# Half of a projection moved ahead, one wait added, and two banks for the last two tiles of a four-block network on one core

## The chip, the cores and the metric

The kernel runs on one NeuronCore of a Trainium2 chip, as one launch. The metric is the device time of the launch in microseconds, lower is better. The core has TensorE (PE, with its weight loads shown as PEld), VectorE (DVE), ScalarE (ACT), GpSimd (POOL), and SyncE (SP), which here issues nearly all DMAs. Each engine executes its own queue in order. They are tied together by semaphores that are waited on by value (`wait_ge`) and raised by instructions when they end (`then_inc`).

## The reference

Four blocks over a residual stream `x` of 1024 tokens by 256 channels, in float32:

```python
x = x + _layernorm(_L0_attn_ref(_layernorm(x), ...))   # softmax attention, 16 heads of 16
x = x + _layernorm(_L0_ffn_ref(_layernorm(x), ...))    # 8 experts, weights by a "golden zone"
x = x + _layernorm(_L1_attn_ref(_layernorm(x), ...))   # linear attention, 16 heads of 128
x = x + _layernorm(_L1_ffn_ref(_layernorm(x), ...))    # top 4 of 16 experts, and a shared one
```

The change touches the third block and the end of the fourth. The third, cut to its core:

```python
q, k, v = h @ Wq, h @ Wk, h @ Wv
beta, gate = sigmoid(h @ Wb + bb), silu(h @ Wg)
q = layernorm(silu(causal_dwconv(q, qconv_w, qconv_b)))    # 4 taps along the tokens, norm per head
k = layernorm(silu(causal_dwconv(k, kconv_w, kconv_b)))
S = (1 - b_t) * S + b_t * (v_t x k_t)                      # per token and head
o_t = S q_t
out = (o * gate) @ Wo
```

The fourth sums the down projections of all experts, weighted per token, over 2816 + 352 hidden rows; each token's sum of 256 channels is then normalised (mean and variance over the channels, eps 1e-5) and added to `x`, which is stored.

## The kernel before

Tokens lie in eight tiles of 128 (`NT = 8`). Channels of the residual stream lie along the free axis in `x` and, turned, along the partitions in `x_parts`. Matrices are multiplied in three matmuls, high x high, high x low, low x high, of operands that are split in two (`matmul3`, L62 to L67): ACT copies the high part to the narrower type, DVE or POOL subtracts it for the low part.

**The linear attention** (class `LinearAttention`, L1705) works head by head in a software pipeline. Head h's queries, keys, values and gates are projected (`project_half`: 512 tokens are six matmuls), convolved, activated, turned (PE transposes), normalised and then used in a chunked form of the recurrence: scores within each tile times a decay matrix `mix`, and states from tile to tile (`state`) times decayed queries `q_dec`. The decays come from one small computation for all heads at the start: logits `z`, their softplus (`exp_logit`, L2151, with the Exp and Ln tables of ACT), three small matmuls that sum them along the tokens (`sum_decay`, L1920), and three ACT operations that bring the sums out of PSUM (`decay_rows`, L2160). From there DVE makes the mix biases (L2340) and SP stores two arrays to DRAM and loads them again, broadcast, per head (`load_mix`, `load_decay`).

The order of each engine's work is written out by hand:

- PE (L2077 on): `finish_first`, the transposes of the first head's queries and keys (`rows_q(0)`, `rows_k(0)`), `sum_decay`, `second_q` (L1956: half of the second head's queries, the transpose of the first head's statistics, the other half), keys and values of the second head, and then the loop over heads: `rows_q`, `turn_k`, `rows_k`, gate, `score` (with the next statistics' transpose in its middle, L2009), `key_values`, the projections of the next head, `outputs`.
- ACT (L2241 on): taps and activations of the first head, `exp_logit`, `decay_rows`, a load of the Silu table, `tap_q(1)` (L2204, the two halves one after the other), `high_gate(0)`, the tap of the second head's keys, `norm_k(0)`, `silu_q(1)`, `copy_v(1)`, `silu_k(1)`, `exp_mix(0)`, and so on.
- DVE (L2476 on): convolutions of the first head, `logits`, `variances` of its queries (L2432: eight statistics, eight aggregates, one sum) with `decay_logs` behind, variances of its keys, `mix_biases`, `copy_stats(0)`, the convolutions of the second head with `shift_k(0)` in between, and so on. In the loop's first round: `probs(0)`, `states(0)`, `shift_k(1)`, the convolution of the third head's queries (L2405), `scale_q(1)` (L2464), the convolution of its keys.
- POOL (L2594 on): low parts of weights, powers for the reciprocal standard deviations, masks of the decay matrices (`mask`, L2547, an affine select over 1024 columns), decayed queries (`decay_q`, L2553), `centre_q` (L2536), the keys' rows. In the loop's first round (`n == 2`): low parts of q, `power`, low parts of k and v, `decay_q(0)`, `centre_q(1)`, `mask(2)`, low part of the gate, `rows_k(1)`, `decay_v(1)`.
- SP (L1844 on): behind `rows_ready` (the end of ACT's `decay_rows`) the stores of the sums, `load_mix(0)`, `store_stats(0)`, `load_norms(0)` (means, then rstds, broadcast from DRAM, for `centre_q` and `scale_q`), and then the loads of each round.

`shift_k` (L2345) is one DVE operation of 128x8 with two SBUF inputs, the keys' negative mean times rstd; `norm_k` on ACT waits for it through `shift_ready`. In L2632 before the change `decay_q(n - 2)` follows with no wait on it.

**The end** (`late_programs`, L2857; class `LastTail`, L2693). The down projections are summed in three passes over the token tiles, `PASSES = ((0, 4), (4, 2), (6, 2))`: tiles 0 to 3, then 4 and 5, then 6 and 7. A pass goes over 25 units (`NTILE`), tiles of hidden rows, and each unit adds `matmul3` for each of its token tiles (`sum_unit`, L3018). Two token tiles of 256 channels share one PSUM bank, `last.acc[j]`. ACT makes the high part of a unit (L3155), DVE the low part of odd units, POOL that of even ones (L3255, L3364). When a pair j of tiles is done, its tail runs: DVE takes statistics of both tiles, aggregates them and adds eps (`dve_first`, L975; `variance`, L960), POOL takes the power -1/2 (`pool_first`, L1007), DVE adds the scaled sums to `x` and makes the shift (`dve_take`, L2697), ACT adds the shift (`act_fix`, L1022), SP stores both tiles, 256 KB (L2997).

## Time and profile before

| | us |
|---|---|
| three runs before, median | 1043.86 |
| their lowest and highest | 1041.45, 1044.31 |
| the profiled execution, its own time | 1039.31 |
| its span, first to last instruction | 1037.5 |
| busy: PE | 1003.8 (97%) |
| busy: DVE, ACT, POOL | 768.5, 675.7, 535.7 |
| mean granted clock of PE, 1 = 2.4 GHz | 0.991 |

The profile is of one execution. Its page has, besides the busy times, the chain of work that ended last; PE has 56% of the span in it, DVE 6%, ACT 3%, POOL 3%. Times in rows count from the start of the span. The duration of a row that ends in xN is that of N instructions together; matmuls are pipelined, so their starts tell more than their durations. In square brackets stand the engine's idle time before the row and what ended it. L12 is line 12 of the kernel before; matmuls are listed at `matmul3`'s lines L65 to L67. `lin_` names belong to the linear attention, `late_` ones to the last block; `s_raw_w_o` is space that the linear attention shares for activated queries and query norms.

### The profile page before, as it was taken

How to read it: one execution, taken by the hardware profiler on the slowest of the kernel's cores; microseconds unless marked ns; L12 is line 12 of the kernel's file. 1: busy time of each engine (PE TensorE's matmuls, PEld its weight loads, DVE VectorE, ACT ScalarE, POOL GpSimd, SP SyncE). 2: the span in 40 equal slices, each digit the busy share in tenths (PEclk: the TensorE clock that was granted, in tenths of full speed). 3: DMA queues.
4: the chain of work that ended last, by engine and by line, in shares of the span. 5: the costliest groups of instructions: out<-in, count | busy, mean ns of one | idle time of the engine just before them, and what ended most of it. 6: DMA issues, size and time to landing. Idle time of an engine off the chain costs nothing.

```text
span 1037.5 us, 19120 instructions
## 1 busy us (share of the span) xinstructions
PE 1003.8 (97%) x6781; PEld 791.5 (76%) x6781; DVE 768.5 (74%) x1579; ACT 675.7 (65%) x1245; POOL 535.7 (52%) x450
## 2 busy tenths in 40 slices
PE   7999999999999998899999999999999999999997
PEld 5333333457887997789989989898898788888997
DVE  5889999646766757899989999999866374434853
ACT  4588888766544446988888888887755353333453
POOL 3351320114069362889889898898334001447553
PEclk9999999999999997999999999999999999999999
DMA  3544443214225201643244223431401124555200
GB/s 96 94 74 65 72 64 65 69 40 145 82 75 151 40 1 31 214 138 108 98 140 172 98 107 125 154 120 67 158 13 40 39 62 119 148 150 152 80 22 21
DMA packets 85931, 96.21 MB, mean 93 GB/s; under 512 B 30169, under 2 KB 68781, under 8 KB 85837
## 3 DMA queue, kind: packets, MB, share of 16 engines
q1 hardware_dynamic: 85104, 94.05, 32.6%
q8 instruction: 54, 0.88, 0.4%
q10 hardware_dynamic: 732, 0.95, 0.4%
q14 instruction: 41, 0.33, 0.1%
HBM read 82.29 MB, written 1.41 MB: 81 GB/s over the span
## 4 chain that ended last, share of the span: by engine, by line
PE 56%; issue 7%; DVE 6%; ACT 3%; POOL 3%; DVEq 2%; DMA 1%; POOLq 0%; SPq 0%; ACTq 0%
PE late_bank L65 8%; PE late_bank L66 8%; PE late_bank L67 8%; PE lin_pair L65 5%; PE lin_pair L67 5%; PE lin_pair L66 5%; PE lin_pair L1917 3%; PE lin_pair L2012 2%; PE lin_pair L2020 2%; PE lin_pair L2030 2%; PE lin_pair L2033 2%; PE gold_bank L65 1%; PE gold_bank L67 1%; PE gold_bank L66 1%; POOL gold_mids L1653 1%
## 5 line engine op out<-in xcount | busy, mean ns | idle before, releaser
L761 ACT ACTIVATE attn_probs<-attn_rows_k 128x512 f32<-128x512 f32 x256 | 138.9, 595 | 24.0 <-PE attn_rows_k L605 19.5
L605 PE MATMUL attn_rows_k<-attn_q_stack,attn_k_stack 50*128 50x512 f32 x256 | 93.8, 445 | 0.2 <-DMA attn_q_stack<-attn_max_rows 0.2
L3273 DVE TENSOR_TENSOR late_mids<-late_mids,late_bank 128x512 f32<-128x512 f32 (+1 forms) x50 | 34.4, 687 | 77.9 <-PE late_bank L67 74.9
L872 DVE TENSOR_REDUCE attn_row_max<-s_sum 128x1 f32<-128x1024 f32 x62 | 75.6, 1220 | 11.0 <-PE attn_rows_q L589 5.0
L618 PE MATMUL attn_ctx<-attn_probs,attn_v 128*32 128x256 f32 x1024 | 81.5, 391 | 0.2
L872 DVE TENSOR_REDUCE attn_row_max<-attn_rows_q 128x1 f32<-128x1024 f32 x62 | 75.9, 1224 | 6.0 <-PE attn_rows_q L589 4.3
L65 PE MATMUL late_bank<-net_x_part_low,late_w_T 128*128 128x512 f32 (+1 forms) x192 | 77.9, 406 | 0.0
L3373 POOL TENSOR_TENSOR late_mids<-late_mids,late_raw_w_T_last 128x512 f32<-128x512 f32 x22 | 29.6, 1368 | 91.1 <-DMA late_raw_w_T_last<-top_weights 91.1
L66 PE MATMUL late_bank<-net_x_part_low,late_w_T 128*128 128x512 f32 (+1 forms) x192 | 76.1, 396 | 0.0
L67 PE MATMUL late_bank<-net_x_part_low,late_w_T 128*128 128x512 f32 (+1 forms) x192 | 76.0, 396 | 0.0
L3183 ACT ACTIVATE late_mids<-late_bank 128x512 f32<-128x512 f32 (+1 forms) x50 | 29.9, 597 | 70.2 <-PE late_bank L67 70.2
L1653 POOL TENSOR_TENSOR gold_mids<-gold_mids,s_later 128x512 f32<-128x512 f32 x27 | 46.8, 1773 | 41.0 <-DMA s_later<-gold_weights 41.0
L2420 DVE SCALAR_TENSOR_TENSOR lin_conv_k<-lin_pair,early_lin_taps,lin_conv_k 128x1021 f32<-128x1021 f32 (+2 forms) x45 | 57.6, 1280 | 2.2
L618 PEld LDWEIGHTS attn_ctx<-attn_probs,attn_v 128*32 128x32 f32 x1024 | 20.2, 108 | 42.3 <-ACT attn_probs L761 30.1
L2218 ACT ACTIVATE lin_normed_k<-lin_pair,lin_k_shift,lin_rstd_k 128x128 f32<-128x128 f32 x128 | 46.3, 472 | 1.9 <-DVE lin_k_shift L2349 1.9
L589 PE MATMUL s_sum<-attn_k_stack,attn_q_stack 48*128 48x512 f32 x124 | 45.4, 444 | 1.7 <-DMA attn_q_stack<-s_part 1.3
L589 PE MATMUL attn_rows_q<-attn_k_stack,attn_q_stack 48*128 48x512 f32 x124 | 45.1, 443 | 0.0
L2030 PE MATMUL lin_pair<-lin_probs,lin_v_rows 128*128 128x128 f32 x240 | 43.9, 275 | 0.0
L605 PEld LDWEIGHTS attn_rows_k<-attn_q_stack,attn_k_stack 50*128 50x128 f32 x256 | 39.3, 184 | 5.3 <-ACT attn_probs L761 3.3
L65 PE MATMUL late_bank<-late_down_T,late_w_T 128*128 128x256 f32 (+1 forms) x152 | 43.2, 284 | 0.0
L3168 ACT ACTIVATE late_w_T<-late_mids 128x256 fp32r<-128x256 f32 (+3 forms) x57 | 27.3, 487 | 24.4 <-PE late_bank L67 23.3
L66 PE MATMUL late_bank<-late_down_T,late_w_T 128*128 128x256 f32 (+1 forms) x152 | 43.0, 283 | 0.0
(496 smaller groups left out, 3514.7 us busy)
## 6 DMA issues: line engine op xcount, KB each, us to landing
s_raw_w_o<-query_norms SPq DMA_DIRECT2D x32, 512.0 KB, 4.9
lin_mix<-decay_sums SPq DMA_DIRECT2D x16, 512.0 KB, 5.8
lin_q_dec<-decay_sums SPq DMA_DIRECT2D x16, 512.0 KB, 6.6
s_later<-gold_weights SPq DMA_DIRECT2D x16, 256.0 KB, 3.4
attn_k_stack<-s_part SPq DMA_DIRECT2D x30, 128.0 KB, 3.5
s_raw_ring<-in_L_ffn_Wg SPq DMA_DIRECT2D x12, 256.0 KB, 2.8
s_raw_ring<-in_L_ffn_Wu SPq DMA_DIRECT2D x12, 256.0 KB, 3.8
attn_k_stack<-s_part SPq DMA_DIRECT2D x33, 64.0 KB, 2.3
```

The costliest lines, as they stand in the source:

```text
L65: pe.matmul(out, w[0], x[0], start=start, stop=False)
L66: pe.matmul(out, w[0], x[1], start=False, stop=False)
L67: return pe.matmul(out, w[1], x[0], start=False, stop=stop)
L589: pe.matmul(ps_tile[tile_bank(n)][:, half * HALF:(half + 1) * HALF], q_stack[rows, h % SLOTS, r * P:(r + 1) * P], k_stack[rows, h % SLOTS, ...
L605: pe.matmul(out, k_stack[rows, h % SLOTS, t * P:(t + 1) * P], q_stack[rows, h % SLOTS, :], start=True, stop=True).then_inc(scored_k, 1)
L618: i = pe.matmul(sums[j * VW:(j + 1) * VW, :], v[:, t, h, :], probs[:, (2 * w + odd) % PB, j * QUARTER:(j + 1) * QUARTER], start=(t == 0), ...
L761: act.activation(probs[:, (2 * k + odd) % PB, side * HALF:(side + 1) * HALF], ring_bank(("exped", 4 * k + n + 1)), ACT.Exp).then_inc(exped, 1)
L872: dve.tensor_reduce(row_max[h % 2][:, tile:tile + 1], ps_tile[tile_bank(n)][:, :], axis=AX, op=ALU.max)\
L1653: pool.tensor_tensor(out, out, weight[v % 4], ALU.mult).then_inc(weighted, 1)
L2030: i = pe.matmul(pair[2][:, cols], self.v_rows[h // 2 % 2][:, c, h % 2, :], self.probs[:, c, :], start=True, stop=(c == 0))
L2218: i = act.activation(self.normed_k[:, c, :], self.tiled[2 if h else 0][:, c, :], ACT.Identity, scale=self.rstd[1][:, c:c + 1], bias=self.k ...
L2420: i = dve.scalar_tensor_tensor(self.conv[m][:, back:T], self.pair[pair][:, 0:T - back], self.taps[:, m, h, j:j + 1], self.conv[m][:, back: ...
```

## The change

Three edits.

1. `second_q` is cut in two. `second_q(0)`, the first half of the second head's queries, stands ahead of `sum_decay`; `second_q(1)`, the statistics' transpose and the other half, behind it. Its wait for the first head's query variances (`q_var`) becomes a wait for the last of the eight statistics reads (`q_read`). On ACT the tap of that half stands ahead of `decay_rows`, under the Exp and Ln tables.
2. In its loop's first round POOL waits for `shift_ready` to be 2, the end of DVE's `shift_k(1)`, before `decay_q(0)`.
3. In the last pass tile 6 is summed in the bank that tiles 6 and 7 shared and tile 7 in the bank of tiles 0 and 1. The first 19 units are done as before, for both tiles; the last six (`APART`) first for tile 6, then for tile 7 (`sum_apart`). The tail of the two tiles is run tile by tile on DVE, POOL and ACT, and SP stores them in two DMAs of 128 KB.

```diff
-        def second_q():
-            pe.wait_ge(self.q_split, 2)
-            pe.wait_ge(self.q_var, 1)
-            self.project_half(pe, "q", 0, pair[3]).then_inc(self.q_half_projected, 1)
-            turn_stats(0)
-            self.project_half(pe, "q", 1, pair[3]).then_inc(self.q_projected, 1)
+        def second_q(half):
+            if half == 0:
+                pe.wait_ge(self.q_split, 2)
+                pe.wait_ge(self.q_read, 1)
+                self.project_half(pe, "q", 0, pair[3]).then_inc(self.q_half_projected, 1)
+            else:
+                turn_stats(0)
+                self.project_half(pe, "q", 1, pair[3]).then_inc(self.q_projected, 1)
...
         rows_k(0)
+        second_q(0)
         sum_decay()
-        second_q()
+        second_q(1)
         project_k(1)
...
         exp_logit()
+        tap_q(1, (0,))
         decay_rows()
         act.add_instruction(mybir.InstLoadActFuncSet(act_func_set_id=SILU, name=act.bass.get_next_instruction_name()))
-        tap_q(1)
+        tap_q(1, (1,))
         high_gate(0)
...
             for c in range(NT):
-                dve.bn_stats(self.stats[m][:, c, :], self.tiled[pair][:, c, :])
+                i = dve.bn_stats(self.stats[m][:, c, :], self.tiled[pair][:, c, :])
+            if h == 0 and m == 0:
+                i.then_inc(self.q_read, 1)
...
                 if n > 2:
                     mask(n)
+            if n == 2:
+                pool.wait_ge(self.shift_ready, 2)
             decay_q(n - 2)
...
+        def sum_acc(tile):
+            return last.acc[tile // 2][:, tile % 2, :] if tile + 1 < NT else last.acc[0][:, 0, :]
...
+                if p == 2 and n == 0:
+                    pe.wait_ge(last.shifted, 1)
...
+            def sum_apart():
+                for n in range(NTILE - APART, NTILE):
+                    sum_ready(2, n)
+                    i = sum_products(2, n, 0)
+                i.then_inc(tile_summed, 1)
+                for n in range(NTILE - APART, NTILE):
+                    i = sum_products(2, n, 1)
+                i.then_inc(tile_summed, 1)
...
             for p in range(len(PASSES)):
-                for n in range(NTILE):
+                for n in range(NTILE if p < 2 else NTILE - APART):
                     sum_unit(p, n)
+            sum_apart()
...
-            last.dve_first(dve, 3, sum_used, 3 * NTILE)
-            last.dve_take(dve, 3, tail.x_fixed)
+            last.dve_first_tile(dve, NT - 2, sum_acc(NT - 2), tile_summed, 1)
+            last.dve_take_tile(dve, NT - 2, sum_acc(NT - 2), tail.x_fixed)
+            last.dve_first_tile(dve, NT - 1, sum_acc(NT - 1), tile_summed, 2)
+            last.dve_take_tile(dve, NT - 1, sum_acc(NT - 1), tail.x_fixed)
...
-            last.pool_first(pool, 3)
+            last.pool_first_tile(pool, NT - 2)
+            last.pool_first_tile(pool, NT - 1)
```

The new functions of `LastTail` do for one tile what those before do for two:

```python
    def dve_first_tile(self, dve, t, src, summed, count):
        one = slice(t, t + 1)
        dve.wait_ge(summed, count)
        dve.bn_stats(self.stats["first"][:, t, :], src)
        dve.drain()
        dve.bn_aggr(self.mean_var["first"][:, t, :], self.stats["first"][:, t, :])
        dve.drain()
        dve.tensor_scalar(self.var_eps["first"][:, one], self.mean_var["first"][:, one, 1], EPS, None, ALU.add)\
            .then_inc(self.first_var, 1)

    def dve_take_tile(self, dve, t, src, x_free):
        one = slice(t, t + 1)
        dve.wait_ge(self.first_rstd, t - 2)
        dve.wait_ge(x_free, self.JOBS)
        dve.scalar_tensor_tensor(self.x[:, t, :], src, self.rstd["first"][:, one], self.x[:, t, :], ALU.mult, ALU.add)
        dve.scalar_tensor_tensor(self.shift["first"][:, one], self.mean_var["first"][:, one, 0], -1.0, self.rstd["first"][:, one],
                                 ALU.mult, ALU.mult).then_inc(self.shifted, 1)

    def act_end_tile(self, act, t):
        act.wait_ge(self.shifted, t - 2)
        act.activation(self.x[:, t, :], self.x[:, t, :], ACT.Identity, bias=self.shift["first"][:, t:t + 1])\
            .then_inc(self.x_fixed, 1)
```

## Rows read from the trace of the kernel before

**Rows 1.** Waits of PE, 446 to 1031 us (total, times, longest)

```profile
PE lin_pair L1917 <- DVE lin_conv_k L2420: 1.6, 2, 1.4
...
PE late_bank L1037 <- ACT late_mids L1018: 0.3, 1, 0.3
```

**Rows 2.** Busy time of one stretch (length, PE busy, PEclk, DMA share, GB/s)

```profile
406.84:411.20 4.36, 4.36 (x14) 0.50 0.07 17
```

**Rows 3.** PE in order of time, 404 to 413 us (start us, us)

```profile
404.11 1.94 PE L1917 MATMUL lin_pair<-net_ident,lin_conv_k 128*128 128x128 f32 x8 [1.32 <-ACT lin_v_rows L2238]
...
406.84 0.79 PE L1925 MATMUL lin_pair<-lin_probs 128*128 128x128 f32 x2 [0.78 <-DVE lin_probs L2337]
...
408.13 0.77 PE L65 MATMUL lin_pair<-net_x_part_low,lin_part_q 128*128 128x512 f32 x1
...
410.84 0.41 PE L1945 MATMUL lin_pair<-net_ident,lin_mean_var_q 128*16 128x128 f32 x1
...
412.64 0.39 PE L65 MATMUL lin_pair<-net_x_part_low,lin_part_k 128*128 128x512 f32 x1
```

**Rows 4.** ACT in order of time, 409 to 422 us

```profile
409.15 1.28 ACT L2251 ACT_TABLE_LOAD   x1
...
412.84 0.78 ACT L2209 ACTIVATE lin_conv_q<-lin_pair,early_lin_taps 128x512 f32<-128x512 f32 x1 [0.92 <-PE lin_pair L67]
...
415.65 1.21 ACT L2201 ACTIVATE lin_conv_k<-lin_pair,early_lin_taps 128x1024 f32<-128x1024 f32 x1 [1.73 <-PE lin_pair L67]
...
421.45 1.06 ACT L2230 ACTIVATE lin_conv_k<-lin_conv_k 128x1024 f32<-128x1024 f32 x1
```

**Rows 5.** Query norms: their loads, and the landing of the first

```profile
415.84 0.81 SPq L1841 DMA_DIRECT2D s_raw_w_o<-query_norms  x2
...
DMA to landing us min/median/max: 4.1/4.1/4.1
```

**Rows 6.** POOL in order of time, 422 to 442 us

```profile
422.07 2.35 POOL L2539 TENSOR_TENSOR lin_acted<-lin_acted,s_raw_w_o 128x1024 f32<-128x1024 f32 x1
...
427.89 1.66 POOL L2534 TENSOR_TENSOR lin_mean_var_q<-lin_var_eps_q,net_neg_half 128x8 f32<-128x8 f32 x1
...
435.46 2.41 POOL L2557 TENSOR_TENSOR lin_q_dec<-lin_q_dec,lin_q_T 128x1024 f32<-128x1024 f32 x1
...
440.17 1.10 POOL L2550 TENSOR_SCALAR_AFFINE_SELECT lin_mix<-lin_mix 128x1024 f32<-128x1024 f32 x1
```

**Rows 7.** DVE in order of time, 435 to 447 us

```profile
435.49 2.40 DVE L2349 SCALAR_TENSOR_TENSOR lin_k_shift<-lin_mean_var_k,lin_rstd_k 128x8 f32<-128x8 f32 x1
...
441.84 1.21 DVE L2468 TENSOR_TENSOR s_raw_w_o<-s_raw_w_o 128x1024 f32<-128x1024 f32 x1
...
442.97 3.99 DVE L2420 SCALAR_TENSOR_TENSOR lin_conv_k<-lin_pair,early_lin_taps,lin_conv_k 128x1021 f32<-128x1021 f32 x3
```

**Rows 8.** The shift two heads on, and the POOL operation beside it

```profile
476.15 0.68 DVE L2349 SCALAR_TENSOR_TENSOR lin_k_shift<-lin_mean_var_k,lin_rstd_k 128x8 f32<-128x8 f32 x1
...
476.08 0.73 POOL L2519 TENSOR_TENSOR lin_part_k<-early_lin_w_k,lin_part_k 128x256 fp32r<-128x256 f32 x1
```

**Rows 9.** The end on POOL, DVE and ACT, 1025 to 1035 us

```profile
1025.70 0.74 POOL L2944 TENSOR_TENSOR late_w_T<-late_mids,late_w_T 128x256 fp32r<-128x256 f32 x1 [0.70 <-ACT late_w_T L3168]
...
1030.96 0.76 DVE L962 BATCH_NORM_STATS2 late_tail_stats_first<-late_bank 128x6 f32<-128x256 f32 x2 [5.60 <-PE late_bank L67]
...
1032.37 0.70 POOL L1005 TENSOR_TENSOR late_tail_rstd_first<-late_tail_var_eps_first,net_neg_half 128x2 f32<-128x2 f32 x1 [5.93 <-DVE late_tail_var_eps_first L967]
...
1033.10 0.88 DVE L2702 SCALAR_TENSOR_TENSOR net_x<-late_bank,late_tail_rstd_first,net_x 128x256 f32<-128x256 f32 x2 [0.81 <-POOL late_tail_rstd_first L1005]
...
1034.08 0.91 ACT L1024 ACTIVATE net_x<-net_x,late_tail_shift_first 128x256 f32<-128x256 f32 x2 [8.46 <-DVE late_tail_shift_first L972]
```

**Rows 10.** Us to landing: the four 256 KB stores; the 8 KB stores of statistics

```profile
DMA to landing us min/median/max: 2.1/2.1/2.2
...
DMA to landing us min/median/max: 1.3/1.4/3.4
```

More of the change, by code:

```diff
@@ L2996, in sp_program @@
             rows = store.rearrange("(c p) d -> p c d", p=P)
-            for j in range(Tail.JOBS):
-                sp.wait_ge(last.x_fixed, j + 1)
-                sp.dma_start(rows[:, 2 * j:2 * j + 2, :], x[:, 2 * j:2 * j + 2, :]).then_inc(stored, 16)
-            sp.wait_ge(stored, 16 * Tail.JOBS)
+            ends = [slice(2 * j, 2 * j + 2) for j in range(Tail.JOBS - 1)] + [slice(t, t + 1) for t in (NT - 2, NT - 1)]
+            for n, tiles in enumerate(ends):
+                sp.wait_ge(last.x_fixed, n + 1)
+                sp.dma_start(rows[:, tiles, :], x[:, tiles, :]).then_inc(stored, 16)
+            sp.wait_ge(stored, 16 * len(ends))
         def pe_program(pe):
@@ L3027, in sum_unit, with sum_products @@
                     pe.wait_ge(sum_low_pool, low_count(SUM_DVE, p, n, False))
+            def sum_products(p, n, c):
                 _, parts = sum_source(p, n)
[L3029 to L3035 removed]
+                rows, tile = slice(0, TILE_ROWS[n]), PASSES[p][0] + c
+                return matmul3(pe, sum_acc(tile), [q[:, c * P:(c + 1) * P] for q in parts], [w[rows, TILES[n], :] for w in down_T],
+                               n == 0 and (p == 2 or tile % 2 == 0), n == NTILE - 1 and (p == 2 or tile % 2 == 1))
+            def sum_unit(p, n):
+                sum_ready(p, n)
+                for c in range(PASSES[p][1]):
+                    i = sum_products(p, n, c)
+                i.then_inc(sum_used, 1)
+            def sum_apart():
[6 more added lines that the diff above has]
+                i.then_inc(tile_summed, 1)
             def turn(i):
@@ L3248, in act_program @@
                         last.act_end(act, 2)
-            last.act_end(act, 3)
+            last.act_end_tile(act, NT - 2)
+            last.act_end_tile(act, NT - 1)
         def dve_program(dve):
```

24 lines of the change are left out of this document (15 added, 9 removed).

## The prediction

> **What bounds the kernel now.** I read the page's chain first (PE has 56% of it), then the waits of PE alone. From 446 us to the end of the matmuls PE waits 5.4 us in six groups, of which [rows 1] has the first and the last. So whatever moves PE earlier at 447 us moves the end by the same, and only two places are left where time is to be had: the start of the linear attention (402 to 447 us), where PE idles and runs slowly, and the 6.6 us behind the last matmul. The three edits lie in these. The granted clock over 406.84 to 411.20 is 0.50, the lower level of 1.2 GHz, though PE issues without a gap [rows 2]. PE did before: the transposes at 404.11 behind a wait of 1.32 us, a gap of 0.78, the decays' sums at 406.84, half a projection of queries at 408.13 [rows 3]. Past 411.2 it is at 2.4 GHz: the keys' twelve matmuls of 512 columns from 412.64 are over before ACT's tap at 415.65 [rows 4], 0.235 us each, while the six from 408.13 to 410.84 take 0.45 [rows 3].
>
> **Edit 1: half of the second queries ahead of the sums.** The transposes' last issue is at about 404.11 + 8 x 0.215 = 405.8. The half's other waits (the split weights, the read statistics) are then over, so its six matmuls fill the gap. They delay the sums; that delay is the price. I work it out at both ends of the clock.
> Clock up by 408.0: the half is issued at 408.3, the sums take half of 1.29 us (406.84 to 408.13), their result is there at 409.2. ACT taps the half from 408.7 to 409.4 (0.78 for half a tap, [rows 4]), then does its three decay rows (0.6 us: from the sums' end at 408.5 to the table load at 409.15) and is done at 410.0, 0.9 later than before. The table load of 1.28 ends at 411.3. PE's second half is issued from 409.1 to 410.5 and ends at 410.9, so the second tap, which started at 412.84 after 0.92 of waiting for PE, starts at 411.3 behind the table load: 1.5 earlier. The keys' tap, at 415.65 behind 1.73 of waiting for PE, comes 2.1 earlier.
> Clock low until 411.4 as before: half 405.8 to 408.5, sums to 409.8 and there at 410.1, rows done at 410.7 (1.6 later), table at 412.0, second half ended at 412.4: only 0.4 earlier.
> From the keys' tap ACT runs on without a wait up to its activation of the keys at 421.45 [rows 4], which also needs DVE's convolution that ended at 421.4; DVE follows the second tap. So this point moves by 1.5 or 0.4. SP's queue is behind the decay rows too: it stores the sums, loads a decay row, stores the statistics and then issues the norms' loads at 415.84, the first landing 4.1 later at 419.9 [rows 5]. With 0.9 more that is 420.8. POOL's centring started at 422.07 [rows 6] and would be free 2.0 earlier, at 420.1; it now waits for the load until 420.8 and gains 1.25. The power of the query variances at 427.89 follows it and ends at 429.55, which let go the statistics' transpose in the middle of PE's scores. So the scores' end, and the states behind them, gain 1.3 in the first case and 0.4 in the second. In the second case the load lands at 421.5 just when POOL wants it. PE issues in the new order without a gap from 404.11 on instead of from 406.84 on, so I expect the clock earlier and take 1.3 (range -0.5 to 1.6: nothing is left if the norms land 1.3 later still, and beyond that it costs).
>
> **Edit 2: POOL waits for the shift.** In the trace DVE's shift of 128x8 takes 2.40 us (435.49 to 437.89), beside POOL's decay of the queries (435.46 to 437.87) [rows 6, 7]. Two heads later it takes 0.68 and ends at 476.83, with POOL's operation beside it at 476.81 [rows 8]. So the shift was held until POOL was done. With the wait, the shift takes about 0.2 and POOL starts at 435.7 instead of 435.46; behind it in POOL's queue stand the centring, the third mask, the gates' low part and the keys' rows, each 0.3 later. DVE's query convolution starts 1.4 earlier, but the scaling behind it needs POOL's centring, which now ends at 440.5, and the mask (1.10 us, at 440.17 before) [rows 6] starts with that end. Before, the scaling at 441.84 [rows 7] came after the mask was over (441.27); now it would meet it. The trace has no mask beside a DVE operation with two SBUF inputs. One bound is no contact: scaling at 440.6, 1.25 earlier. The other is what the shift met: held until the mask ends at 441.5, 0.3 earlier. Both operations read 1024 columns, as in the rows where DVE was held, so I take 0.3; below that, -0.3 if the mask or the scaling starts as much later as POOL's other work. The keys' convolution (442.97, 3.99) follows, and PE waited for it 1.4 us [rows 1, 7]: that wait passes the gain on, and PE has enough of it for 1.25.
> The Trainium skill, SBUF — State Buffer, section Who interferes with whom, says that a DVE instruction with two SBUF inputs contends with a GpSimd instruction that reads SBUF, and that the later one is blocked fully. By that rule the mask holds the scaling and the edit brings 0.3; without it 1.25. The held shift agrees with it (2.40 against 0.2); no row shows a mask doing it.
>
> **Edit 3: last two tiles in a bank each.** The number of matmuls stays. The last six units of both tiles (36 matmuls at 0.12, before the statistics at 1030.96, so from 1026.6) are done tile by tile, so tile 6 is whole 18 x 0.12 = 2.2 us before the end, at 1028.8. The low parts that this needs earlier were all ready when POOL's last ended at 1025.70 + 0.74 = 1026.4 [rows 9], and the bank of the last tile was free long before, so PE doesn't wait. What ends the kernel is then the chain of one tile instead of two: statistics 0.76 for two, pitch 0.34 saved; aggregates 0.1; POOL's power 0.70 for two columns against 1.66 for eight [rows 6], so 0.16 a column, 0.16 saved (bounds 0 and 0.35); the scale-and-add 0.88 for two, 0.40 saved; ACT's fix 0.91 for two, 0.40 saved. The last store is 128 KB: 256 KB land in 2.1 and 8 KB in 1.4 [rows 10], so 0.3 saved (bounds 0 and 0.7). Sum 1.7 (1.3 to 2.2). Tile 6's own chain goes by 1030.9 on DVE, when tile 7's statistics start (1030.96), and its store is issued at 1031.5: both clear of the last tile's.
>
> **The sum.** 1.3 + 0.3 + 1.7 = 3.3 us. The profiled execution took 1039.31 (span 1037.5): it becomes 1036.0. The median of the runs before is 1043.86, 4.5 above the profile; 3.3 less is 1040.5. I forecast that median. What can be told from no change is 0.3%, or 3.1 us: the forecast lies just beyond.
>
> **Rivals.**
> a) The mask doesn't hold the scaling: edit 2 gives 1.25, total 4.25, 1039.6. For it: the mask has one input, the rows that show holding have two. Against: the same reading of SBUF.
> b) The clock rises no earlier: edit 1 gives 0.4, total 2.4, 1041.5. For it: the clock stayed at 0.50 for 4.36 us of unbroken issue [rows 2]. Against: 2.7 us more of it now.
> c) The linear attention gives back both: a later wait of PE, on DVE or POOL, grows by as much. Only the end's 1.7 is left, 1042.2. Against: the waits of [rows 1] are short; it takes a queue that doesn't move with PE.
> d) Slower: PE stays at 1.2 GHz until the second values. Place: half 1 and the twelve matmuls of keys. They then end at 418.1 + 0.4 and the keys' tap is at 418.5 instead of 415.65, +2.9, which ACT's gapless chain hands to the scores. With 0.3 and 1.7 back that is +0.9, 1044.8. It decides once the clock rises after about 414.5 and so eats more than edits 2 and 3 give. For it: 0.50 over the whole of [rows 2] shows that unbroken issue alone doesn't bring the clock at once. Against: it did come then, and in the new order the unbroken issue begins 2.7 us sooner.
>
> **How the numbers follow.** Forecast 0.42, its own range 1038.5 to 1042; a) 0.20; b) 0.20; c) 0.12; d) 0.06. The range takes in all but d) and the tail of a), and the scatter of a median among runs that lay between 1039.3 and 1044.3: 1037.0 to 1042.9. Faster by over 0.3% (below 1040.7): half of the forecast's cases and some (0.24), most of a) (0.17), a few of b) and c) (0.09): 0.50. Slower (above 1047.0) needs d) and a bad median: 0.05. The rest, 0.45, is within.
>
> **What would show it.** Of edit 1: the half's six matmuls from 405.8, no PE gap, the clock up before 409, the second tap at 411.3, the decay rows done at 410.0, the norms landed before POOL wants them, the scores 1.3 earlier. Wrong, if the second tap is near 412.4 or POOL idles for the norms. Of edit 2: a shift of 0.2, then POOL's decay, the scaling ending with a duration above 2 or starting late at the mask's end; wrong, if it takes 1.2 right behind the centring. Of edit 3: statistics of tile 6 2.2 us ahead of tile 7's, and 2.6 us instead of 4.0 from the last tile's statistics to the end of ACT's fix (1030.96 to 1034.99 before); wrong, if PE waits among the last 36 matmuls.

## The result, and the profile after

The kernel after took 1037.28 us (median of 8 runs, 1034.97 to 1038.84) against 1042.53 for the kernel before on the same chip (8 runs): ratio 0.9945, 95% interval 0.9925 to 0.9965. By the ratio that is 5.7 us faster (the medians differ by 5.2), where 3.3 was forecast; the forecast time was 1040.5. Runs more than 1.5% above the fastest of their kernel, as one of 1098.7 here, are left out of every ratio, and the profile of the third comparison, whose execution took 1059.09 us, is used only where it is named. Two later comparisons gave 0.9966 (0.9941 to 0.9991) and 0.9954 (0.9938 to 0.9970). The three together say 4.7 us less (the mean ratio 0.9955 of 1042).

The profiled execution took 1035.81 us, its span 1034.1. All that follows is counted from a mark ahead of the change, the start of ACT's copy of the first head's values (402.96 before, 402.45 here). The parts ahead of it, which the edits don't touch, differ from one execution to the next: in the sixteen profiles below the mark lies between 402.45 and 410.87 us.

PE in order of time, answering to [rows 3]:

```profile
403.60 1.06 PE L1918 MATMUL lin_pair<-net_ident,lin_conv_k 128*128 128x128 f32 x8 [2.04 <-ACT lin_v_rows L2243]
404.42 0.48 PE L65 MATMUL lin_pair<-net_x_part_low,lin_part_q 128*128 128x512 f32 x1
...
406.75 0.63 PE L1926 MATMUL lin_pair<-lin_probs 128*128 128x128 f32 x2
...
408.09 0.57 PE L65 MATMUL lin_pair<-net_x_part_low,lin_part_q 128*128 128x512 f32 x1
...
409.68 0.40 PE L65 MATMUL lin_pair<-net_x_part_low,lin_part_k 128*128 128x512 f32 x1
```

The half is issued from 404.42 to 406.75 and the decays' sums follow at 406.75, 4.30 after the mark; before they stood at 3.88. PE was already at its upper clock when the transposes of the keys began (0.82 us from 403.60 to 404.42; at the lower level they take 1.59, from 404.86 to 406.45 in the kernel with ACT's old order below). So the half started early enough to delay the sums by only 0.42, although the clock was low again over most of the half and over all of the sums (1.27 us from 406.75 to 408.02, 1.29 before). ACT, answering to [rows 4]:

```profile
407.05 0.78 ACT L2214 ACTIVATE lin_conv_q<-lin_pair,early_lin_taps 128x512 f32<-128x512 f32 x1 [1.53 <-PE lin_pair L67]
...
408.90 1.28 ACT L2257 ACT_TABLE_LOAD   x1
410.19 0.78 ACT L2214 ACTIVATE lin_conv_q<-lin_pair,early_lin_taps 128x512 f32<-128x512 f32 x1
...
412.69 1.21 ACT L2205 ACTIVATE lin_conv_k<-lin_pair,early_lin_taps 128x1024 f32<-128x1024 f32 x1 [1.42 <-PE lin_pair L67]
...
418.79 1.06 ACT L2235 ACTIVATE lin_conv_k<-lin_conv_k 128x1024 f32<-128x1024 f32 x1 [0.24 <-DVE lin_conv_k L2426]
```

The first half is tapped (407.05) while the sums are still being made. The table load comes 6.45 after the mark (before 6.19), the second tap stands right behind it at 7.74 (before 9.88), the keys' tap at 10.24 (before 12.69), the activation of the keys at 16.34 (before 18.49): 2.15 earlier. POOL, answering to [rows 6], and DVE, answering to [rows 7]:

```profile
419.76 2.35 POOL L2547 TENSOR_TENSOR lin_acted<-lin_acted,s_raw_w_o 128x1024 f32<-128x1024 f32 x1 [0.63 <-DMA s_raw_w_o<-query_norms]
...
425.58 1.65 POOL L2542 TENSOR_TENSOR lin_mean_var_q<-lin_var_eps_q,net_neg_half 128x8 f32<-128x8 f32 x1
...
433.07 2.40 POOL L2565 TENSOR_TENSOR lin_q_dec<-lin_q_dec,lin_q_T 128x1024 f32<-128x1024 f32 x1 [0.23 <-DVE lin_k_shift L2355]
...
437.79 1.10 POOL L2558 TENSOR_SCALAR_AFFINE_SELECT lin_mix<-lin_mix 128x1024 f32<-128x1024 f32 x1
```

```profile
432.83 0.16 DVE L2355 SCALAR_TENSOR_TENSOR lin_k_shift<-lin_mean_var_k,lin_rstd_k 128x8 f32<-128x8 f32 x1
...
437.87 2.10 DVE L2476 TENSOR_TENSOR s_raw_w_o<-s_raw_w_o 128x1024 f32<-128x1024 f32 x1
439.89 3.98 DVE L2426 SCALAR_TENSOR_TENSOR lin_conv_k<-lin_pair,early_lin_taps,lin_conv_k 128x1021 f32<-128x1021 f32 x3
```

POOL waits 0.63 for the norms, as forecast, and its decay for the shift, which takes 0.16. The scaling takes 2.10: it starts at 437.87, beside the mask of 437.79, and ends at 439.97, 1.1 after the mask's end at 438.89. The keys' convolution starts 37.44 after the mark (before 40.01). The waits of PE, answering to [rows 1]:

```profile
PE lin_pair L1918 <- DVE lin_conv_k L2426: 3.0, 4, 1.3
...
PE late_bank L1037 <- ACT late_mids L1018: 0.3, 1, 0.3
```

The wait for DVE's convolution of the keys has grown from 1.6 to 3.0 us (from 446 us before, from 443 here, so that the wait at 447 and at 444 us is in both). Its four parts are 1.25 at 444 us and 1.30, 0.28 and a small one at later heads: part of the gain is given back at 550 and 677 us (below). The tail, on DVE and then on ACT, answering to [rows 9]:

```profile
1027.11 0.43 DVE L2723 BATCH_NORM_STATS2 late_tail_stats_first<-late_bank 128x6 f32<-128x256 f32 x1 [3.44 <-PE late_bank L67]
...
1029.27 0.43 DVE L2723 BATCH_NORM_STATS2 late_tail_stats_first<-late_bank 128x6 f32<-128x256 f32 x1
...
1030.85 0.48 DVE L2740 SCALAR_TENSOR_TENSOR net_x<-late_bank,late_tail_rstd_first,net_x 128x256 f32<-128x256 f32 x1 [0.67 <-POOL late_tail_rstd_first L2733]
```

```profile
1031.44 0.51 ACT L2746 ACTIVATE net_x<-net_x,late_tail_shift_first 128x256 f32<-128x256 f32 x1 [1.65 <-DVE late_tail_shift_first L2741]
```

The statistics of tile 6 start at 1027.11, those of tile 7 at 1029.27, 2.16 later. From there to the end of ACT's fix it is 2.68 us (before 4.03), to the end of the span 4.83 (before 6.54): 1.71 saved.

### The profile page after: what moved, and what is told of

It reads as the page before. It is cut to its first block, busy times and chain, and to the rows that moved or that the text cites. A ratio compares the mean times of both kernels' runs of the same rounds, so it can differ in the third digit from the quotient of the medians.

```text
span 1034.1 us, 19129 instructions
## 1 busy us (share of the span) xinstructions
PE 999.6 (97%) x6781; PEld 788.4 (76%) x6781; DVE 766.9 (74%) x1581; ACT 675.3 (65%) x1245; POOL 535.9 (52%) x451
## 4 chain that ended last, share of the span: by engine, by line
PE 52%; DVE 8%; issue 7%; POOL 4%; DMA 4%; DVEq 2%; ACT 2%; SPq 0%; POOLq 0%
PE late_bank L65 8%; PE late_bank L66 8%; PE late_bank L67 8%; PE lin_pair L65 4%; PE lin_pair L67 4%; PE lin_pair L66 4%; PE lin_pair L1918 3%; PE lin_pair L2015 2%; PE lin_pair L2023 2%; PE lin_pair L2033 1%; DVE lin_conv_k L2426 1%; DMA s_raw_w_o<-query_norms 1%; PE gold_bank L65 1%; PE gold_bank L67 1%; PE gold_bank L66 1%
```

## The experiments

Each kernel was timed in five rounds beside the kernel before. The table has the ratio, and from each kernel's profile the start of a few instructions counted from the mark: ACT's second table load, ACT's activation of the second head's keys, DVE's convolution of the third head's keys, PE's transposes of the normed keys (they wait for that convolution). "Clock" is the mean granted clock over the 9 us from the mark. "Boundaries" is what PE lost at later heads, above all at 550 us: how much more than 231.82 us lies between these transposes and the same ones of the head at 680 us. That is the shortest distance in any profile, in the second of the kernel after. "Tail" goes from the last tile's statistics to the end of the span.

| kernel | ratio (95%) | clock | table | keys | conv. | turned | boundaries | tail |
|---|---|---|---|---|---|---|---|---|
| before | | 0.53 | 6.19 | 18.49 | 40.01 | 44.15 | 0.3 | 6.54 |
| before, again | 1.0006 (0.9991-1.0020) | 0.53 | 6.19 | 18.44 | 39.95 | 44.09 | 2.4 | 6.53 |
| edit 2 | 1.0008 (0.9996-1.0019) | 0.69 | 6.21 | 18.62 | 39.72 | 43.85 | 0.1 | 6.54 |
| edit 3 | 0.9993 (0.9981-1.0005) | 0.74 | 6.81 | 18.65 | 41.08 | 45.22 | 1.3 | 4.83 |
| edits 2, 3 | 0.9980 (0.9961-0.9999) | 0.64 | 6.19 | 18.84 | 41.13 | 45.25 | 1.3 | 4.85 |
| edit 1 | 0.9986 (0.9964-1.0007) | 0.81 | 6.47 | 16.36 | 37.88 | 42.01 | 0.0 | 6.61 |
| edits 1, 2 | 0.9983 (0.9970-0.9996) | 0.90 | 6.20 | 16.21 | 37.33 | 41.46 | 2.1 | 6.61 |
| edits 1, 3 | 0.9954 (0.9940-0.9968) | 1.00 | 5.49 | 15.49 | 37.02 | 41.15 | 1.2 | 4.86 |
| after | 0.9945, 0.9966, 0.9954 | 0.81 | 6.45 | 16.34 | 37.44 | 41.57 | 1.8 | 4.83 |
| after, again | (the middle one) | 0.89 | 6.22 | 16.23 | 37.32 | 41.45 | 0.0 | 4.81 |
| after, ACT's old order | 0.9970 (0.9951-0.9989) | 0.71 | 6.84 | 17.39 | 40.07 | 44.20 | 1.2 | 4.78 |
| after, keys' half first | 0.9946 (0.9928-0.9964) | 1.00 | 5.48 | 15.48 | 36.59 | 40.71 | 1.0 | 4.82 |
| after, statistics stored first | 0.9962 (0.9945-0.9980) | 1.00 | 5.49 | 15.49 | 37.78 | 41.90 | 1.3 | 4.85 |
| after, mask behind gate | 0.9952 (0.9934-0.9970) | 0.92 | 6.21 | 16.22 | 38.53 | 42.67 | 1.7 | 4.83 |
| after, all three moved | 0.9944 (0.9929-0.9960) | 1.00 | 5.48 | 15.48 | 35.70 | 39.84 | 0.4 | 4.86 |
| the same, again | 0.9949 (0.9934-0.9964) | 1.00 | 5.48 | 15.49 | 35.72 | 39.86 | 2.2 | 4.79 |

**One edit each, on the kernel before.** Edit 1:

```diff
-        sum_decay()
-        second_q()
+        second_q(0)
+        sum_decay()
+        second_q(1)
...
+        tap_q(1, (0,))
         decay_rows()
```

> The kernel before with edit 1 alone (half of the second queries ahead of the decays' sums, on PE and ACT). Theory A (the step was mis-sized: PE's clock was at its upper level behind the gap at 404 us in the profile after, at its lower one before, and which of the two a run meets is not the edit's doing): the keys' activation of the second head starts 2.1 us earlier against the start of the stage where the clock is up by 405, 0.4 to 1.3 earlier where it isn't; the time falls by 1.0 to 2.1 us. Theory B (the prediction's): 1.3 us whatever the clock, POOL's centring then waits for the norms. Theory C (edit 1 is worth more than either, since the medians differ by 5.7 us and edit 3 can give only 1.7): 3.5 us or more.

Edit 2:

```diff
+            if n == 2:
+                pool.wait_ge(self.shift_ready, 2)
             decay_q(n - 2)
```

> The kernel before with edit 2 alone (POOL waits for VECTOR's shift before the first decayed queries). Theory A: the shift takes 0.2 us, the scaling behind it is held by the mask (about 2.1 us instead of 1.2), the keys' convolution starts 0.3 to 0.5 us earlier, the time is the same within its interval. Theory B (the mask holds nothing): 1.25 us earlier, the time 1.2 us less. Theory C (GpSimd's later decay makes the second head's rows late): nothing or slower by up to 0.3.

Edit 3:

```diff
-            last.dve_first(dve, 3, sum_used, 3 * NTILE)
-            last.dve_take(dve, 3, tail.x_fixed)
+            last.dve_first_tile(dve, NT - 2, sum_acc(NT - 2), tile_summed, 1)
+            last.dve_take_tile(dve, NT - 2, sum_acc(NT - 2), tail.x_fixed)
+            last.dve_first_tile(dve, NT - 1, sum_acc(NT - 1), tile_summed, 2)
+            last.dve_take_tile(dve, NT - 1, sum_acc(NT - 1), tail.x_fixed)
```

> The kernel before with edit 3 alone (the last two token tiles in a bank each, finished one by one). Theory A: from the last tile's statistics to the end of the span 4.8 us instead of 6.5, so 1.7 us less in the time. Theory C (edit 3 holds the surplus of the 5.7 us): over 3 us less, with a difference in the trace ahead of 1026 us to show for it.

The times alone settle little: 1.5 us less, 0.8 more, 0.7 less, each with an interval over 2 us wide. The profiles do. With edit 1 the keys' activation is at 16.36, without it at 18.62 and 18.65. With edit 2 the shift takes 0.16 and the scaling 2.10, and between the keys' activation and the convolution's result there are 25.23 us instead of 25.65 (turned less keys), so 0.42 saved. That is so in the profiles whose scores ran at the upper clock and whose POOL power was not held; edit 2 can also cost time, as the experiment on the mask shows. With edit 3 the tail is 4.83. Theory A holds for edits 2 and 3. For edit 1 its upper case holds (2.1 earlier); its smaller case (0.4 to 1.3 at the lower clock) was met in no profile: the least is 1.68, in the third profile of the kernel after.

**Pairs.**

```diff
 edits 1 and 2: the kernel after with the tail of before
 edits 2 and 3: the kernel after without
-        second_q(0)
         sum_decay()
-        second_q(1)
+        second_q()
 edits 1 and 3: the kernel after without
-            if n == 2:
-                pool.wait_ge(self.shift_ready, 2)
```

> The kernel before with edits 1 and 2, the tail as before. Theory A (each edit is worth what its piece of the trace shows, whatever stands beside it): 2.2 + 0.4 = 2.6 us less at PE's transposes of the normed keys (447 us), counted from the start of the values' copy of the first head; the time 1.5 to 2.6 less, as the head boundaries at 540 and 667 us may take 0 to 1.5. Theory B (the edits need each other; alone they measured 1.5, -0.8 and 0.7): 4 us or more together.

> The kernel after without edit 1. Theory A: the stage before 447 us as in the kernel before less 0.4, the tail 1.7 shorter; time 1.0 to 2.1 less than before. Theory B (edits need each other): no gain, as the single ones' sum (-0.1).

> The kernel after without edit 2 (GpSimd doesn't wait for the shift). Theory A: the shift takes 2.2 to 2.4 us again, 0.4 is lost at the keys' convolution; time 2.5 to 3.9 less than before. Theory B: under 2 less, since edit 2 is needed for the others' gain to pass.

They measured 1.8, 2.1 and 4.8 us less. Comparing kernels that differ in one edit alone (four such pairs for each edit, with the mean of 0.9945 and 0.9966 for the kernel after, and 0.001 of ratio worth 1.04 us) edit 1 is worth 2.7 us, edit 3 2.5 and edit 2 0.2. Nothing speaks for edits that need each other: the differences from 2.2, 1.7 and 0.4 are within what the intervals allow.

**The kernels before and after once more.** No edit.

> The kernel after once more, beside the kernel before on the chip of the single edits. Theory A (the first comparison's kernel before ran high by chance: its median was 1042.5 there and 1040.7 over 29 runs here): 3.3 to 4.0 us less than the kernel before, as the parts in the traces add up (2.2, 0.4 and 1.7, less what the head boundaries give back). Theory B (the three together are worth more than the sum of the single ones, which measured 1.5, -0.8 and 0.7): 5 us or more.

> The kernel before itself, for a second profile of it. Theory A (a run's places differ by where the lower clock falls and by what lands late, whatever the kernel): from the values' copy to the keys' activation 18.5 to 18.9 us again, to PE's transposes of the normed keys 44.1 to 45.3; the time the same as the kernel before. Theory B (the first profile was a slow one at this place, and edit 1 brings less): 17.5 or less to the keys' activation.

> The kernel after a third time. Theory A (2.2 to 3.1 for edit 1, 0.3 to 0.5 for edit 2, 1.7 for edit 3, less up to 1.8 at the head boundaries): 3.5 to 5.0 us less than before; 16.2 to 16.4 us from the values' copy to the keys' activation, or 15.5 where PE's clock stays up over the sums. Theory B (the prediction's sum): 3.3 us, with about 17.2 to the keys' activation.

The second profile of before has the same 18.4 and 44.1 as the first, though its mark lies 7 us later: the place wasn't slow by chance. Of the first comparison's 5.7 us about one is scatter, by the mean of the three.

**Who sets the scores: ACT or POOL?**

```diff
 the kernel after with
-        tap_q(1, (0,))
         decay_rows()
         (table load)
-        tap_q(1, (1,))
+        tap_q(1)
```

> The kernel after, with PE's new order, but ACT taps both halves behind the decay rows and the table load, as before. Theory A (edit 1 is worth what ACT gains by having half a tap in front of the table load: ACT's chain from the table load to the keys' activation sets the scores): the second tap starts 0.7 to 0.8 us later than in the kernel after and the query transpose's scaling by as much; the time is 0.7 more. Theory B (POOL and the norms set the scores, as the prediction had it): no loss, since POOL waits for the norms anyway.

PE of this kernel, and then ACT:

```profile
406.45 0.77 PE L65 MATMUL lin_pair<-net_x_part_low,lin_part_q 128*128 128x512 f32 x1
...
409.05 0.38 PE L1926 MATMUL lin_pair<-lin_probs 128*128 128x128 f32 x2
```

```profile
410.55 1.28 ACT L2256 ACT_TABLE_LOAD   x1
411.85 1.44 ACT L2214 ACTIVATE lin_conv_q<-lin_pair,early_lin_taps 128x512 f32<-128x512 f32 x2
...
414.25 1.21 ACT L2205 ACTIVATE lin_conv_k<-lin_pair,early_lin_taps 128x1024 f32<-128x1024 f32 x1 [0.65 <-PE lin_pair L67]
...
421.10 1.06 ACT L2235 ACTIVATE lin_conv_k<-lin_conv_k 128x1024 f32<-128x1024 f32 x1 [0.99 <-DVE lin_conv_k L2425]
```

PE's order is the new one, and still the keys' activation is at 17.39 instead of 16.34: the two taps behind the table load take 1.44, 0.66 more than one, and the load itself is 0.39 later. Only the 0.66 is the order of ACT; the 0.39 comes from PE, which in this profile was at its lower clock over the transposes and the half (2.74 to 5.34 after the mark, 1.97 to 4.30 in the kernel after). In all profiles in which POOL's power of the query variances was not held (see the end) ACT's scaling of the transposed queries (what PE's scores wait for) follows the keys' activation by 5.81 to 5.83 us, gapless; POOL's wait for the norms doesn't show in it. So ACT, and ahead of it DVE's convolution, sets the start of the scores, not POOL. The numbers further on hold other things too (POOL's power was held here, and the scores ran at the lower clock), so only those up to the keys are used.

```diff
 the kernel after with
+        store_stats(0)
         sp.wait_ge(self.rows_stored, 32)
         load_mix(0)
-        store_stats(0)
         load_norms(0)
```

> The kernel after, with the first head's statistics stored ahead of SP's wait for the decay rows, so the norms are read 0.5 to 2 us earlier. Theory A (ACT sets the scores): POOL's centring loses its wait of 0.3 to 0.8 us, the scores don't move, the time is the same. Theory B (the prediction's: POOL behind the norms sets the scores): they move by 0.6 and the time by 0.6.

POOL's wait for the norms is gone, its power of the query variances is at 21.63 instead of 23.13 after the mark (0.85 of that is the clock's, as for the keys), and the scaling of the queries follows the keys' activation by 5.82 as ever. So POOL doesn't set the scores' start, theory A. PE's scores of this kernel:

```profile
433.46 1.67 PE L2015 MATMUL lin_pair<-lin_q_T,lin_k_T 128*128 128x128 f32 x8 [2.08 <-ACT lin_q_T L2181]
```

They start 0.85 us earlier than in the kernel after, but behind a wait of 2.08 instead of 0.77 us and at the lower clock, and that takes the gain back: DVE's shift is at 30.72, where the kernel after has 30.38. Edits 1 and 3 without edit 2 show the same wait, the same 1.67 and the same 30.72.

**The sums at the upper clock.** PE's gap ahead of the transposed keys is filled with half of the next projection:

```diff
 the kernel after with
         rows_q(0)
+        second_k_half()       # six matmuls, moved from project_k(1)
         rows_k(0)
```

> The kernel after, with half of the second head's key projection in PE's gap ahead of the transposed keys (six matmuls of 512 columns, moved forward). Theory A (the sums on PE, then ACT's decay rows, set the stage): the sums start when VECTOR's logs are there, 0.4 us earlier, and end 1.0 earlier where the clock stays up; the keys' activation and the scores 0.5 to 1.0 earlier, the time by as much. Theory B (VECTOR's statistics and logs or the table load set it): no gain. Against both: at the lower clock the six matmuls take 2.6 us, 0.6 more than the gap, and delay the transposes, 0.6 slower.

ACT of this kernel:

```profile
409.09 1.28 ACT L2263 ACT_TABLE_LOAD   x1
410.39 0.78 ACT L2220 ACTIVATE lin_conv_q<-lin_pair,early_lin_taps 128x512 f32<-128x512 f32 x1
...
411.37 1.21 ACT L2211 ACTIVATE lin_conv_k<-lin_pair,early_lin_taps 128x1024 f32<-128x1024 f32 x1
...
419.09 1.06 ACT L2241 ACTIVATE lin_conv_k<-lin_conv_k 128x1024 f32<-128x1024 f32 x1 [1.86 <-DVE lin_conv_k L2432]
```

The table load is at 5.48, the second tap at 6.78, the keys' activation at 15.48: 0.86 earlier than after, in the range of theory A. The keys' tap no longer waits for PE, and the activation waits 1.86 for DVE's convolution: up to there the keys' own projection being early brings nothing, the clock, which never falls up to and over the sums, brings it all. Two profiles without the move have the clock and the 15.49 too. Further on the move does differ from them: PE's scores follow a wait of 0.33 and run at the upper clock,

```profile
426.19 1.16 PE L2020 MATMUL lin_pair<-lin_q_T,lin_k_T 128*128 128x128 f32 x8 [0.33 <-ACT lin_q_T L2187]
```

and DVE's shift is at 29.52, against 30.72 in those two; so it is in all three profiles with the move. The rows of busy time over the 9 us from the mark (length; busy time of PE, weight loads, DVE, ACT, POOL; granted clock; DMA share; GB/s) for before and after:

```profile
402.96:411.96 9.00, 7.07 (x25) 5.74 (x26) 5.84 (x39) 5.68 (x10) 3.28 (x2) 0.53 0.06 15
```

```profile
402.45:411.45 9.00, 7.85 (x35) 6.65 (x36) 6.69 (x39) 6.76 (x12) 3.38 (x3) 0.81 0.06 15
```

A mean over 9 us hides where the lower clock lies. The same rows from 6 to 8 us after the mark, before and after:

```profile
408.96:410.96 2.00, 2.00 (x7) 1.32 (x6) 0.49 (x4) 1.46 (x3) 1.54 (x1) 0.50 0.12 33
```

```profile
408.45:410.45 2.00, 2.00 (x10) 1.58 (x10) 1.43 (x6) 1.97 (x5) 1.54 (x1) 1.00 0.06 14
```

There the clock is 0.50 in all five profiles of kernels without edit 1 and 1.00 in all eleven with PE's new order. In which state a profile comes to the transposes, 1.15 us after the mark, is not the edit's doing, for both states occur with and without it. So like is compared with like (us after the mark, without the profiles of the keys' move):

| clock at the transposes | without edit 1 | with PE's new order |
|---|---|---|
| lower, and it stays so | up at 8.4 (before, twice) | up at 5.2 (ACT's old order; the third profile of after) |
| lower, up at 1.2 to 2.1 | falls again at 4.7 to 5.5, up at 8.1 to 8.9 (edit 2; edit 3) | stays up (edits 1 and 2; after, again; mask behind gate) |
| upper | falls at 2.4, up at 9.2 (edits 2 and 3) | falls at 2.4, up at 5.8 (edit 1; after), or never falls (edits 1 and 3; statistics stored first) |

In each row the filled gap brings the clock back about 3 us sooner or keeps it up. Whether the keys' half adds to that is open: all three profiles with it stayed up, but they came at the upper level, where two of four with edit 1 alone did so too.

**Does the mask hold the scaling?**

```diff
 the kernel after with
-                if n == 2:
-                    mask(2)
                 low("gate", self.wg[(n - 1) % 2], self.g_high, self.g_split, n)
+                if n == 2:
+                    mask(2)
```

> The kernel after, with the third mask of GpSimd behind the low part of the gates instead of ahead of it. Theory A (the mask holds VECTOR's scaling of the queries until it is over): the scaling takes 1.2 us instead of 2.1, the keys' convolution starts 0.9 earlier, PE's wait for it at 444 us shrinks by as much and the time falls by 0.9 against the kernel after, unless a later wait takes it. Theory B (the scaling is slow behind the centring for another reason, as the memory's write before it): 2.1 us as before, no gain.

DVE, then POOL, of this kernel:

```profile
440.77 1.23 DVE L2476 TENSOR_TENSOR s_raw_w_o<-s_raw_w_o 128x1024 f32<-128x1024 f32 x1 [0.69 <-POOL s_raw_w_o L2547]
441.91 3.99 DVE L2426 SCALAR_TENSOR_TENSOR lin_conv_k<-lin_pair,early_lin_taps,lin_conv_k 128x1021 f32<-128x1021 f32 x3
```

```profile
438.34 2.40 POOL L2547 TENSOR_TENSOR s_raw_w_o<-s_raw_w_o 128x1024 f32<-128x1024 f32 x1
440.85 1.74 POOL L2527 TENSOR_TENSOR lin_part_gate<-lin_w_gate,lin_part_gate 128x256 fp32r<-128x256 f32 x1
442.54 1.10 POOL L2558 TENSOR_SCALAR_AFFINE_SELECT lin_mix<-lin_mix 128x1024 f32<-128x1024 f32 x1
```

The scaling takes 1.23, right behind the centring, and the gates' low part, issued beside it, takes 1.74 (its shortest run in this kernel 0.72) and ends 0.6 after the scaling. From the shift to the convolution it is 6.18 us (6.18 and 6.19 with all three moves) against 7.06 after: 0.88 less. Theory A for the mask. The forecast for the convolution and the time isn't borne out by this run: its convolution comes 1.1 later after the mark than in the kernel after, with POOL's power held (see the end) and half of the scores at the lower clock, and the time stayed within the scatter of the kernel after.

The mask can also make edit 2 cost time. The kernel with edits 1 and 3 and the one with the statistics stored first differ by edit 2 (and by the store, which moved nothing up to there): both have the shift at 30.72. Mask and scaling of the first, then of the second:

```profile
438.25 1.10 POOL L2558 TENSOR_SCALAR_AFFINE_SELECT lin_mix<-lin_mix 128x1024 f32<-128x1024 f32 x1
```

```profile
439.91 1.22 DVE L2476 TENSOR_TENSOR s_raw_w_o<-s_raw_w_o 128x1024 f32<-128x1024 f32 x1
```

```profile
446.55 1.09 POOL L2558 TENSOR_SCALAR_AFFINE_SELECT lin_mix<-lin_mix 128x1024 f32<-128x1024 f32 x1
```

```profile
446.63 2.09 DVE L2476 TENSOR_TENSOR s_raw_w_o<-s_raw_w_o 128x1024 f32<-128x1024 f32 x1 [0.70 <-POOL s_raw_w_o L2547]
```

Without edit 2 POOL had begun its decay 1.21 us ahead of the shift and the mask was over before the scaling began; with it POOL waited 1.42 for the shift, and the mask met the scaling. The convolution is at 37.02 without edit 2 and at 37.78 with it: here the edit costs 0.76. Edits 2 and 3 alone, whose scores ran at the lower clock as well, agree: turned less keys is 26.41 there and with the statistics stored first, and 25.66 with edits 1 and 3.

**All three moves.**

```diff
 the kernel after with the three diffs above: keys' half first,
 third mask behind the gates' low part, statistics stored first
```

> The kernel after with all three further moves: half of the second keys' projection in the gap ahead of the transposed keys, the third mask behind the gates' low part, the statistics stored ahead of the wait for the decay rows. Theory A (the first saves 0.8 to 1.0 on PE and ACT, the second 0.9 on VECTOR, the third nothing): PE's transposes of the normed keys 1.3 to 1.9 us earlier than in the kernel after, and the time 1 to 2 less than that kernel's. Theory B (from some point PE's own work or GpSimd's rows bind there): no better than the better of the two alone.

> The kernel with the three further moves once more, beside the kernel after. Theory A: 1 to 2 us less than the kernel after; 15.5 us from the values' copy to the keys' activation, 39.8 to PE's transposes of the normed keys, where the kernel after has 41.5. Theory B (scatter): no less than the kernel after.

```profile
434.65 0.16 DVE L2361 SCALAR_TENSOR_TENSOR lin_k_shift<-lin_mean_var_k,lin_rstd_k 128x8 f32<-128x8 f32 x1
...
439.69 1.23 DVE L2482 TENSOR_TENSOR s_raw_w_o<-s_raw_w_o 128x1024 f32<-128x1024 f32 x1
440.83 3.99 DVE L2432 SCALAR_TENSOR_TENSOR lin_conv_k<-lin_pair,early_lin_taps,lin_conv_k 128x1021 f32<-128x1021 f32 x3
```

PE's transposes are at 39.84 and 39.86, 1.6 to 1.7 earlier than in the two profiles of the kernel after in the table, as theory A has it. The times are 5.8 and 5.3 us less than before, 0.9944 and 0.9949, where the kernel after has a mean of 0.9955. But the intervals overlap, the kernel after itself had 0.9945 once, and beside it in the same rounds the second run gained only 0.5 (0.9949 against 0.9954): the 1 to 2 us less in the time that theory A asked for are not shown.

## Why the prediction was wrong

The measured median, 1037.28, lies below the forecast's own range (1038.5 to 1042); only the wider one, which adds the scatter of a median, takes it in.

**What bounds the kernel.** Right: gains before 447 us reach the end, less what the head boundaries take, and that is taken from the kernel before too (0.3 and 2.4 in its two profiles). 

**Edit 1: the step that failed.** The term of 1.3 us was mis-sized: at the keys' activation it is 2.15 in the first profile of the kernel after, and the same 2.15 at DVE's shift behind the scores (32.53 before, 30.38 after). Two steps of its working were off.

The first is the delay of the sums: the decay rows "done at 410.0, 0.9 later than before", and with them the second tap only 1.5 earlier. In the table's profiles with edit 1's full order the table load, which follows the rows, came 0.0 to 0.3 later (6.20 to 6.47 against 6.19), or 0.7 earlier where the clock never fell; the second tap of the first profile came 2.14 earlier. I had taken the transposes' end (405.8) and the half's pace from the one profile I had, in which PE was at 1.2 GHz over the whole stretch. So the half was forecast from 2.84 to 5.34 after the mark, and it ran from 1.97 to 4.30. The forecast of a clock that rises over the half and halves the sums was not met either: the sums ran at the lower clock, 1.27 against 1.29. It was the earlier start of the half that paid here, and PE's clock at the transposes, which gave it, stands ahead of the edit. The second profile of the kernel after gains as much in another way: its half waits for the statistics until 2.93, but it and the sums (4.62) run at the upper clock, and the keys' activation is at 16.23. Where the forecast's pattern did occur, its working holds: with ACT's old order the half ran from 2.74 to 5.34, the sums at the upper clock, and the table load came 0.65 later; in the third profile of the kernel after the second tap came 1.65 earlier and the keys' activation 1.68.

The second is the limit by the norms: POOL's centring "now waits for the load until 420.8 and gains 1.25". POOL does wait 0.63, but its centring comes 1.80 earlier, and the scores' start hangs on ACT's chain, which gives the full 2.15; POOL's power, 1.8 earlier, costs PE 0.23 in the middle of the scores, and the states behind them start 2.08 earlier. The keys' tap was forecast 2.1 earlier and came 2.45.

Where the clock never falls the keys' activation gains 3.0 (18.49 less 15.49), but that isn't edit 1's worth: in both such profiles without the keys' move PE then waits 2.08 for the scores, runs them at the lower clock, and the shift keeps 1.81 of it.

**Edit 2.** Right in place and price for the kernel it was read from: 0.42 against 0.3, with the scaling held by the mask as said. Not foreseen is that the same hold makes it cost 0.76 where POOL would have been ahead of DVE. SBUF — State Buffer, section Who interferes with whom, in the Trainium skill, gave this by its rule; the mask moved away (1.23 instead of 2.10) shows it in this kernel. Rival a), that the mask doesn't hold the scaling, is out.

**Edit 3.** Right: 1.71 against 1.7, no wait among the last matmuls.

**The sum and the other rivals.** With the measured 2.15, 0.42 and 1.71 the sum is 4.3, and the three comparisons' mean is 4.7. The profile's own time, forecast at 1036.0 and measured at 1035.81, was right only since two things cancelled: 0.85 more from edit 1 and 0.5 ahead of the mark stand against 1.5 more given back at the boundaries; that is luck. Rivals b) (the clock rises no earlier) and d) (it stays low until the second values) are refuted by the clock between 6 and 8 us after the mark, 1.00 with edit 1 and 0.50 without. Rival c) (a later wait gives all back) exists as a mechanism, but no profile shows it as a consequence of the change: the kernel after gave back 1.8 us in its first profile and nothing in its second, the kernel before 0.3 and 2.4. Of the absolute miss (1040.5 against 1037.28) 1.3 us are the median of before, 1043.86 over three runs and 1042.53 over eight.

## What to carry to other kernels

Before pricing a moved matmul by the profile's pace, ask what the move does to the idle stretch ahead: here filling it brought the clock back about 3 us sooner, or kept it up. And don't take the pace of one profile for the kernel's: how late the half came depended on the clock that PE had already, 0.82 or 1.59 us for the transposes ahead of it. An upper clock at one place can also be paid for at the next wait. When two queues both seem to lead to the same point, find the gapless chain to it (here 5.82 us on ACT) before letting the slower one cap the gain. With a mark that lay anywhere from 402.45 to 410.87 us, count from a mark next to the change in several profiles; total times of five rounds could not rank edits of 0.4 to 2 us.

## What the runs showed of the hardware

**A code packet in the way of a small store.** At each head SP stores the query statistics (8 KB) and then issues the norms' loads. SP of the kernel after and of the kernel with edit 1, at the same head:

```profile
534.51 0.34 SPq L1835 DMA_DIRECT2D query_norms<-lin_stat_rows  x1
538.02 0.81 SPq L1842 DMA_DIRECT2D s_raw_w_o<-query_norms  x2
```

```profile
538.04 0.34 SPq L1835 DMA_DIRECT2D query_norms<-lin_stat_rows  x1
539.43 1.38 SPq L1842 DMA_DIRECT2D s_raw_w_o<-query_norms  x2
```

3.51 against 1.39 from the store's issue to that of the loads. In all sixteen profiles the instruction queue has one packet of 16 KB beside this store. Where it is first seen 1.0 us behind the store's issue (seven profiles, read in slices of 0.1 us) the loads followed the store by 3.05 to 3.52, where it is seen at 1.2 or later (four) by 1.36 to 1.40; at 1.1 both occur (1.38 and 1.39, 3.16 to 3.50). The norms land 4 to 5 us after their loads, POOL's centring, DVE's scaling and the convolution follow, and PE waits for them up to 1.4 us at 550 us when the store was slow. That the packet is the cause is inferred from the timing, and no kernel was made to move it.

**GpSimd and VECTOR hold each other both ways.** Usually DVE's scaling of the first head's queries is first and holds POOL. In the kernel with edit 3 alone POOL's keys' rows came first:

```profile
426.26 2.32 DVE L2442 TENSOR_SCALAR lin_var_eps_q<-lin_mean_var_q 128x8 f32<-128x8 f32 x1
428.50 1.21 DVE L2468 TENSOR_TENSOR lin_acted<-lin_acted,s_raw_w_o 128x1024 f32<-128x1024 f32 x1
```

```profile
426.16 2.39 POOL L2568 TENSOR_TENSOR lin_k_rows<-lin_k_rows,early_norm_row 128x1024 f32<-128x1024 f32 x1 [0.16 <-issue]
428.66 2.55 POOL L2534 TENSOR_TENSOR lin_mean_var_q<-lin_var_eps_q,net_neg_half 128x8 f32<-128x8 f32 x1
```

An addition over 128x8 took 2.32 us instead of 0.19 before, until POOL's operation of 1024 columns was over, and then the scaling held POOL's power: 2.55 instead of 1.65. ACT's scaling of the queries came 0.9 later. Which of the two starts first at this place differed between profiles (POOL's first in three of sixteen: edit 3, ACT's old order, mask behind gate).
